# Routing spread over the units, pages opened as images arrive, and images stored inside the expert stage

## The reference

```
x = x + attention(ln_c(x))        # q, k l2-normalized; softmax(q k^T * temperature) v; projection
t = tokens(x)
s = softmax(ln(t) @ gate_w + gate_b)            # 4 experts
keep the 2 largest of s per token, divide them by their sum
t = t + sum over the 2 experts of gate * (gelu(ln(t) @ w1[e] + b1[e]) @ w2[e] + b2[e])   # hidden 768
out = t as (16, 192, 32, 32)
```

## Time and profile before

| | us |
|---|---|
| three runs | 2817.43, 2823.03, 2830.2; median 2823.03 |
| profiled execution | 2849.2 (span 2846.6) |
| setup | 0 to 38.65 |
| next image's jobs without attention | 38.65 to 109.5 |
| attention, images 0 to 15 | 109.5 to 1755.4 |
| last projections, routing, table, first rows | 1755.4 to 1813.1 |
| expert stage | 1813.1 to 2770.2 |
| output stage | 2770.2 to 2846.6 |

### The profile page before, as it was taken

The page is one execution under the profiler, slowest core; times in us unless marked ns, Lnnn a source line. Parts: engine busy times, 40 slices in busy tenths (PEclk is TensorE's granted clock), DMA queues, the critical chain, the costliest instruction groups (busy, mean ns, idle before and its releaser), DMA issues. The chain is left out here.

```text
span 2846.6 us, 58847 instructions
## 1 busy us (share of the span) xinstructions
PE 2505.1 (88%) x18693; PEld 1321.8 (46%) x18693; DVE 1710.0 (60%) x4886; ACT 1786.6 (63%) x2228; POOL 1406.2 (49%) x1136
## 2 busy tenths in 40 slices
PE   4699889889889888888888887599999999999975
PEld 2334333333333333333333322377777777777754
DVE  6557666666666666666666656555555555555522
ACT  2487677667667667667677675355556555655542
POOL 2334435435425434434434432477777777777750
PEclk9799999999999999999999999799999999999997
DMA  3211111111111111111111133444444444444419
GB/s 87 56 50 41 46 45 47 45 46 51 41 46 50 43 48 51 39 49 51 40 49 52 39 114 129 177 150 172 162 160 168 151 175 156 167 161 159 175 62 334
DMA packets 160274, 276.40 MB, mean 97 GB/s; under 512 B 21552, under 2 KB 129552, under 8 KB 150576
## 3 DMA queue, kind: packets, MB, share of 16 engines
q1 hardware_dynamic: 141648, 245.37, 26.8%
q0 software_dynamic: 13344, 27.87, 2.7%
q10 hardware_dynamic: 5056, 0.42, 0.3%
HBM read 174.07 MB, written 49.59 MB: 79 GB/s over the span
## 5 line engine op out<-in xcount | busy, mean ns | idle before, releaser
L784 ACT ACTIVATE probs<-ps_s 128x1024 f32<-128x1024 f32 x1024 | 1013.6, 1022 | 335.7 <-PE ps_s L683 329.5
L1351 POOL TENSOR_TENSOR h_split<-h_f,h_split 128x512 f16<-128x512 f32 x444 | 552.3, 1244 | 237.1 <-ACT h_f L1328 230.1
L696 PE MATMUL ps_o<-probs,v_aug 128*32 128x512 f32 x4096 | 573.6, 634 | 0.6 <-ACT probs L784 0.6
L1046 POOL TENSOR_TENSOR inv_norm<-sumsq,minus_half 128x16 f32<-128x16 f32 x128 | 375.2, 2932 | 401.1 <-DVE sumsq L989 400.8
L1278 PE MATMUL ps_h<-m_xn_t,packs 128*128 128x512 f16 x2220 | 552.6, 380 | 0.5 <-DVE m_xn_t L1413 0.5
L1324 ACT ACTIVATE h_split<-ps_h,packs 128x512 f16<-128x512 f32 x444 | 305.1, 687 | 391.5 <-PE ps_h L1278 391.5
L1292 PE MATMUL ps_y<-packs,h_split 128*128 128x192 f16 x5328 | 511.9, 245 | 0.8 <-POOL h_split L1351 0.8
L1292 PEld LDWEIGHTS ps_y<-packs,h_split 128*128 128x128 f16 x5328 | 452.9, 97 | 105.8 <-POOL h_split L1351 2.2
L683 PE MATMUL ps_s<-stacks_odd 98*128 98x512 f16 x1024 | 320.0, 399 | 27.1 <-DMA stacks_odd<-heads 23.3
L683 PE MATMUL ps_s<-even 98*128 98x512 f16 x1024 | 318.9, 397 | 22.8 <-DMA even<-heads 18.7
L1328 ACT ACTIVATE h_f<-ps_h,packs 128x512 f32<-128x512 f32 x444 | 301.7, 679 | 0.0
(11 more groups left out here) (213 smaller groups left out, 2883.0 us busy)
## 6 DMA issues: line engine op xcount, KB each, us to landing
packs<-expert_pack SPq DMA_DIRECT2D x74, 1635.0 KB, 6.9
even<-heads SPq DMA_DIRECT2D x192, 96.0 KB, 2.4
stacks_odd<-heads SPq DMA_DIRECT2D x192, 96.0 KB, 2.4
tile_rows<-sorted_rows SPq DMA_DIRECT2D x37, 400.0 KB, 6.6
tokens<-in_x_dram SPq DMA_DIRECT2D x17, 768.0 KB, 5.5
y_in<-y_tokens SPq DMA_DIRECT2D x16, 768.0 KB, 8.9
out_dram<-y_out SPq DMA_DIRECT2D x16, 768.0 KB, 7.1
even<-heads SPq DMA_DIRECT2D x128, 48.0 KB
```

Of the source, the lines that this page charges most:

```text
L696: mm = pe.matmul(ps_o[32 * j:32 * j + 32, f, :], v_aug[:, par, m, g * GH + j, :], probs[:, (GH * p + j) % PRING, f * HALF:(f + 1) * HALF], ...
L784: act.activation(probs[:, u % PRING, :], ps_s[:, u % 2, :, :].rearrange("p f n -> p (f n)"), ACT.Exp).then_inc(s_probs, 1)
L1046: pool.tensor_tensor(inv_norm[:, t, :], sumsq[:, t, :], minus_half[:, :], ALU.pow).then_inc(s_inv, 1)
L1351: pool.tensor_tensor(h_split[:, n % HSPLIT, 1, :], h_f32[:, n % HBUF, :], h_split[:, n % HSPLIT, 0, :], ALU.subtract).then_inc(s_h, 1)
```

## The change

Four things are changed together.

1. The table of units. `X_UNITS` start at unit 1 (before 2), rounds are 4.5 units apart (before 5), the last projection spreads to unit 63, and routing has one more stage, since `gates` is split into `ranks` (unit 10) and `gates` (unit 13). The mean and variance of the next image come in unit 9, ahead of the ranks, and the first two normalizations ahead of the gates. The puts stand in eight units of their own, 19 to 30, on two semaphores (lower and upper half). In the last image the late routing moves from units 45-63 to 35-54, and its projection runs two jobs per unit.
2. Pages. `sorted_rows` is now a list of 37 pages of 512 rows. A pair of experts gets a new page when its last one is full, so pages fill in the order of the images. This is computed in each image's placing block (`row_places`), and each row carries its two experts as integers. The end table and job `z` are gone; SP reads the experts of a tile from the page's first row in DRAM (`load_pack`), and the whole list is filled in setup, by one DMA that ACT issues.
3. Images inside the expert stage. When tile 2b+8 is under way, all rows of image b are in `y_tokens`. SP loads it; PE transposes it in steps 0 to 3 of the next two tiles into the bank that the rows' transposes use, DVE copies, SP stores. So 14 images are done there.
4. The output stage has the last two images.

```diff
-X_UNITS = tuple(range(2, NT + 2))
-ROUNDS = tuple(range(14, 64, 5))
-POST_UNITS = tuple(range(16, 64, 2))
-LATE_POST_UNITS = tuple(range(20, 44))
+X_UNITS = tuple(range(1, NT + 1))
+ROUNDS = tuple(14 + (9 * r + 1) // 2 for r in range(NT + 2))
+POST_UNITS = tuple(19 + 44 * i // (3 * NT - 1) for i in range(3 * NT))
+LATE_POST_UNITS = tuple(22 + i // 2 for i in range(3 * NT))
...
-EARLY_ROUTE = {"stats": 1, "rstd": 2, "logits": 5, "exp": 6, "gates": 9, "classes": 12, "pairs": 14, "place": 16, "put": 18}
+EARLY_ROUTE = {"stats": 1, "rstd": 2, "logits": 5, "exp": 6, "ranks": 10, "gates": 13, "classes": 15, "pairs": 17,
+               "place": 18, "put": (19, 21, 22, 23, 25, 26, 27, 30)}
...
@@ setup
-            sp.wait_ge(s_fill, 4)
-            for c in range(NPAIR):
-                sp.dma_start(mlp.rows[c * CAP:c * CAP + TROWS, :].rearrange("(p s) w -> p s w", s=SLOT),
-                             rows[:, 0:SLOT, :]).then_inc(s_filled, 16)
+            act.wait_ge(s_fill, 6)
+            act.dma_start(mlp.rows.rearrange("(i p s) w -> p i (s w)", p=P, s=SLOT),
+                          rows[:, 0:SLOT, :].rearrange("p s w -> p (s w)").unsqueeze(1).to_broadcast([P, NTILE, SLOT * ROW])
+                          ).then_inc(s_filled, 16)
-            pool.wait_ge(s_filled, 16 * NPAIR)
+            pool.wait_ge(s_filled, 16)
...
@@ dve_image
-                if u == ROUNDS[0] - 2:
+                if u == ROUNDS[0] - 3:
                     for t in range(2):
                         split_rows(dve, img, t, pre)
...
@@ pool_image
-                if 0 <= u - at["put"] < NT // 2:
-                    for t in range(2 * (u - at["put"]), 2 * (u - at["put"]) + 2):
-                        pool.indirect_dma_start(mlp.rows[:, :], bass.IndirectOffsetOnAxis(ap=index[:, t:t + 1], axis=0),
-                                                rows[:, t, :], None).then_inc(s_scatter, 16)
+                if u in at["put"]:
+                    t = at["put"].index(u)
+                    pool.indirect_dma_start(mlp.rows[:, :], bass.IndirectOffsetOnAxis(ap=index[:, t:t + 1], axis=0),
+                                            rows[:, t, :], None).then_inc(s_scatter[2 * t // NT], 16)
...
@@ expert stage
     def load_pack(sp, i, slot):
-        e = sp.value_load(mlp.table[0:1, 1 + slot, i:i + 1], min_val=0, max_val=NE - 1)
+        named = mlp.rows[i * TROWS:i * TROWS + 1, EXPERT + slot:EXPERT + slot + 1].bitcast(I32)
+        e = sp.value_load(named, min_val=0, max_val=NE - 1)
...
+    def load_image(sp, b):
+        sp.wait_ge(s_put, 16 * SLOT * (2 * b + OUT_LAG - 1))
+        if b:
+            sp.wait_ge(s_t, NT * b)
+        sp.dma_start(y_back[:, :, :], y_img[b]).then_inc(s_in, 16)
+    def store_image(sp, b):
+        sp.wait_ge(s_t_done, NT * (b + 1))
+        sp.dma_start(out_img[b], y_half[:, :, :]).then_inc(s_out, 16)
+    def turn_image(pe, b, t):
+        if t == 0:
+            pe.wait_ge(s_in, 16 * (b + 1))
+        elif t != NT // 2:
+            pe.wait_ge(s_t_done, NT * b + t)
+        for k in range(2):
+            mm = pe.transpose(ps_j[0:HC, k * P:(k + 1) * P], y_back[:, t, k * HC:(k + 1) * HC], ident[:, :])
+        mm.then_inc(s_t, 1)
...
@@ pe_tile, at the end of step n (i, s: image and tile half)
+            if done is not None and n < NT // 2:
+                turn_image(pe, done[0], done[1] + n)
...
@@ SP, tile i
                 for slot in range(2):
                     sp.wait_ge(s_w2, STEPS * i + NK * (slot + 1))
                     load_pack(sp, i + 2, slot)
+                    if slot == 0:
+                        images(sp, i)        # store_image(b - 1), load_image(b) at i = 2 b + 8
```

More of the change, by code:

```diff
@@ L1079, in dve_image @@
             for at, number in routes(img):
[L1080 removed]
+                for stage, step in (("stats", row_stats), ("logits", row_logits), ("ranks", row_ranks), ("gates", row_gates),
                                     ("classes", row_classes), ("pairs", row_pairs)):
@@ L1423, in dve_tile, with images @@
             assert pre.n == TILE_PRE_STEPS, pre.n
+    def images(sp, i):
+        b, half = (i - OUT_LAG + 1) // 2, (i - OUT_LAG + 1) % 2
+        if half == 0 and 1 <= b <= DONE_IMAGES:
+            store_image(sp, b - 1)
+        if half == 0 and 0 <= b < DONE_IMAGES:
+            load_image(sp, b)
     with nc.Block() as block:
@@ L1438, in _ @@
                     load_pack(sp, i + 2, slot)
+                    if slot == 0:
+                        images(sp, i)
+            for i in range(NTILE - 2, NTILE):
+                images(sp, i)
+            sp.wait_ge(s_out, 16 * DONE_IMAGES)
         @block.tensor
@@ L1546, in _ @@
         def _(dve):
-            for b in range(B):
+            for b in range(LEFT):
                 for q in range(0, GROUPS, 2):
```

232 lines of the change are left out of this document (125 added, 107 removed).

## The result

The changed kernel takes 2819.95 us in the median (19 runs, 2815.15 to 2823.4), the kernel before 2832.23 (19 runs, 2817.43 to 2842.22): a ratio of 0.9959, 95% interval 0.9949 to 0.997. A second series gave 2820.64 beside 2826.30, ratio 0.997 (0.9959 to 0.9981). So it is 0.3 to 0.4% faster. The forecast was 2760, its range ended at 2815, and the measured time lies above both.

A forecast was written before the change was run, and what follows sets the result against it. TensorE, 88% busy, was taken as the bound, the output stage as DMA-bound. Attention -86, setup +16, its end -1, experts +28 and +36, output -56 sum to -63: 2786 profiled, 2760 median; range 2695 to 2815.

The forecast's parts named there:

- The baseline: Whole kernel: differences summed against one profiled execution of 2849.2 us, result taken off the median 2823.0, 26 us less.
- Part 1: Attention, image ends: last round starts at unit 55, not 59, so heads come earlier; 3.5 us gained at each of 15.
- Part 2: Attention, next image's means first: 6.2 us of gaps go, a 4.2 us wait for the placing block comes; net 0.3 per image.
- Part 3: Attention, scatters apart: third round's gap and slow clock, 4.0 us, go; 1.8 us of waits come; net 2.2 per image.
- Part 4: Attention, rounds 4.5 units apart instead of 5: PE's work unchanged, taken as 0, bounds +1 to -4 us per image.
- Part 5: Setup: filling all 37 page-table tiles, 15.2 MB, makes GpSimd wait and ends setup at 55 us; +16 us.
- Part 6: End of attention: last image's puts move earlier, so PE's wait for GpSimd goes, while the routing chain grows; -1 us.
- Parts 7 and 8: Expert stage: +28 us for PE's image transposes, +36 us for PE waiting on image loads queued behind a pack.
- The rival without a wait: Expert stage: no wait for the image's load, since the DMA engines have slack; 36 us fewer, 2724; chance 0.20.
- Part 9: Output stage: only two images are left, 20 us for 76.4; -56 us.
- The rival that gave 2823: Attention gains a third, 23 us for 86, as VectorE's backlog drags into GpSimd's tight stretch and gaps change places; chance 0.10.

The follow-up runs named there:

- e8: The changed kernel with the rounds 5 units apart again (first at unit 14, last at 59), everything else as changed: 2842.72 us, 22.8 more.
- e5: The changed kernel with the loop over images 3 to 14 written four images long instead of two, on all engines: 2802.24 us, 17.7 less.
- b_third: The kernel before, unchanged, profiled a third time, in the series of the changed kernel's second: 2829.05 us beside a median of 2826.30.
- e13: The kernel before with only the next image's mean, variance and first two normalizations moved ahead of the gates: 2807.57 us, ratio to before 0.9933.
- e10: The changed kernel with the routed images' placing block cut in two, second half at unit 19, first scatter at unit 20: 2804.86 us, 15.1 less.
- e6: The changed kernel with image 15's eight scatters in units 19 to 26 instead of 19 to 30: 2809.61 us, 10.3 less.
- e3: The changed kernel with SP storing the last image and loading the next ahead of the pack in its queue: 2781.18 us, 38.8 less.
- e9: The changed kernel with no image done inside the expert stage, all 16 in the output stage, which has four load buffers: 2803.56 us.
- b_again: The kernel before, unchanged, for a second profile: 2841.49 us in one execution beside a series of 2846.85.
- e12: The kernel before with the loop over images 3 to 14 four images long instead of two: 2818.99 us beside 2826.30, ratio 0.9961.

## Why the prediction was wrong, step by step

**The baseline: failed.** The sum was made against a profile of 2849.2 us, and a constant 26 us was taken off for the median. But the excess was no constant of profiled executions: the changed kernel's profile took 2818.7 us, its median is 2819.95. The excess lies in the attention stage and is mostly slow clock, behind the one-piece gap of the third round (20.5 us of clock) and at image ends (8.5). Parts 1 and 3 had counted this same clock, 1.7 us a place, as gains. So it was taken off once as a gain of the change and once as the profile's excess. Besides, 2823.0 was the median of three runs, where 19 gave 2832.2, so 9 of the 26 were not even the profile's excess. Taking off the constant makes 26 of the 60 us.

**Part 1, image boundary: failed on the size.** Forecast 3.5 us at each of 15 ends, 52.5 us (its own terms, 2.0 + 1.7, add up to 3.7); e8 measures 1.6, 24 us. PE's idle time at the ends fell by as much, from 36.5 to 12.6 us. The wait for the heads went, but at five ends the loop's jump stays, 2.2 to 2.7 us of idle time (some 4.2 us each in all by e5). And the 1.7 us of clock did not come beside the wait: of the ten ends without a jump, one has it in e8 when the waits are back. The earlier trace rows show image 9, whose end has no jump; its neighbours' gaps of 3.5 and 3.4 us would have told.

**Part 2, means first: mechanism right, net not isolated.** The new wait was named, with its place and releaser, and came at 3.25 to 3.6 us for 4.2. The net of 0.3 us has no run of its own. Parts 2 and 3 together, forecast as 2.5 us per routed image, are what boundaries leave of the measured gain: 105.8 - 101.8 - 1.6 = 2.4 against the first profile, and 104.2 - 101.7 - 1.6 = 0.9 against b_third. So the match depends on the first profile's slow clock, and is luck as far as that goes. The gain of 6.2 us that the net is made of is no gain by itself: e13 gets 1.7 us per image for it, as PE only meets the next wait earlier. e10 shows the block's order to be worth 0.7 to 1.4 us per image.

**Part 3, scatters: right in kind.** The third round's gap went, and 1.8 us of other waits was set against it. Waits of 0.7 to 1.4 us and of 1.2 to 1.4 us came some 40 and 51 us into most routed images, behind VectorE and ScalarE, 2.0 us per image together. That GpSimd's powers cause them was not tested.

**Part 4, closer rounds: 0, as forecast, apart from the boundary.** e8's routed images differ by 1.4 us, which the boundary explains.

**Part 5, setup: failed on the queue.** +16 was forecast for GpSimd's wait, whose end was forecast as about 51.5 and came at 50.9; +24.7 came (+22.4 later), as ScalarE's small stores stood behind the fill. It was named as what would make the prediction wrong ("setup ends near 65"), yet carried no chance in the sum, and the text had put the setup's end before down to VectorE, where ScalarE's last issue ends as late. The fill took 44.3 us from issue to landing for 15.2 MB, 342 GB/s with the other traffic beside it, where the forecast had 37 us by the 407 GB/s of a 6 us stretch. The Trainium skill (DMA: Bandwidth & Descriptors, section Bandwidth) gives about 358 GB/s for a core's HBM, by which the estimate is 42 us; the measured time is nearer to that.

**Part 6: right in the tail (-1.5 for -1)**, but it did not see that image 15 itself gets 7 us longer, as its projection, moved ahead by the late tables, waits for the scatters that stand up to unit 30 (e6).

**Parts 7 and 8, expert stage: right.** 28 + 36 forecast; 25.0 + 34.3 measured (e3). The wait was forecast as 1.9 us and is 26.9 / 13 = 2.07. The rival without a wait is refuted. The register load from DRAM shows no cost in the stage: 945.6 us in e9 against 945.8, with the pack issued 0.18 us later behind its product. The Trainium skill (Runtime: NRT & Kernel Launch, The ~15 us preamble/postamble breakdown) gives about 1.3 us for register loads from HBM; here the whole time from the product's end to the pack's issue is 0.92 us, so the trace shows less.

**Part 9: right**, -60.3 for -56.

From 2760 to 2820: 26 the constant taken off, 28 the image ends (24 for 52.5), 7 image 15, 9 the setup, less 9 for the expert and output stages, make 61. The image ends are e8's figure, against the first profile; with the spread of 11 us between attention stages of the same code it is good to some us, so that the sum closes this well is luck. The rival that gave 2823, a third of the gain, had the time nearly right, but its mechanism (the backlog dragging into GpSimd's stretch) is not what the runs show.

## What to carry to other kernels

Before a profile's excess over the median is taken off as a constant, find in which stage it lies: it may be the very thing that the change removes. Gaps of one stream don't add: removing one brings the engine earlier to the next, so price the last wait of each stretch, not each gap. And look at every gap over all repetitions (odd and even images, first and last) before one of them stands for all.

## What the runs showed of the hardware

- Behind PE's wait of 2.3 us in the third round the granted clock was 1.2 GHz for 3.4 us when the wait stood in one piece (13 images of the first profile and of b_again) and stayed at 2.4 GHz when it was parted into 1.1 and 1.2 us (12 images of b_third). One piece does not always bring it: the five gaps of 2.2 to 2.9 us at the jumps of e10 had none behind them.
- The same program's attention stage took 1645.8 and 1624.2 us with 82.4 and 49.3 us of clock lost: 33 us of lost clock went with 21.6 us of time.
- At the jump back of this loop PE was idle for 2.2 to 2.9 us (3.0 once in e5), and taking out three jumps saved 4.2 us each in the stage. Where a wait for a transfer stood at the same place (e12), it was 1.1 to 3.7 us each.
- A small DMA took 18.85 us to issue from an engine whose queue held one transfer of 15.2 MB, and 1.3 us instead of 0.64 while that transfer ran from another engine's queue.
